# Attention and a two-step expert layer on one core: rows reloaded earlier, gathers one group further ahead, tokens and velocities in one buffer

## The reference

```python
probs = softmax(_gelu(xf @ router_w1 + router_b1) @ router_w2 + router_b2)
topk_p, topk_i = top_k(probs, 2)                   # two of eight experts for each token
v = zeros_like(xf); integrated = xf
for _ in range(2):
    ctx = concatenate([integrated, v], axis=-1)
    x_sh, v_sh = _inl(_gelu(ctx @ shared_w1 + shared_b1) @ shared_w2 + shared_b2, integrated, v, mu)
    ctrl = _experts(ctx_e, flat_idx, expert_w1, expert_b1, expert_w2, expert_b2)
    x_r, v_r = _inl(ctrl, x_e, v_e, mu)            # for both choices, then weighted and summed
    x_next = sw * x_sh + (1.0 - sw) * x_r
    v_next = sw * v_sh + (1.0 - sw) * v_r
    halt = sigmoid(_gelu(integrated @ halt_w1 + halt_b1) @ halt_w2 + halt_b2)
    integrated = integrated + halt * (x_next - integrated)
    v = v + halt * (v_next - v)
refined = _gelu(integrated @ refine_w1 + refine_b1) @ refine_w2 + refine_b2
out = layernorm(xf + (xf + integration_weight * refined))
```

## Time and profile before

| | us |
|---|---|
| median of 3 runs (1504.65 to 1505.9) | 1505.86 |
| the profiled execution, its own time | 1501.05 |
| its span, first to last instruction | 1499.3 |
| VectorE busy in the span | 1052.8 |
| TensorE busy in the span | 1051.0 |
| ScalarE busy in the span | 848.2 |
| GpSimd busy in the span | 500.4 |

### The profile page before, as it was taken

The page is one execution under the profiler, slowest core; times in us unless marked ns, Lnnn a source line. Parts: engine busy times, 40 slices in busy tenths (PEclk is TensorE's granted clock), DMA queues, the critical chain, the costliest instruction groups (busy, mean ns, idle before and its releaser), DMA issues.

```text
span 1499.3 us, 21764 instructions
## 1 busy us (share of the span) xinstructions
PE 1051.0 (70%) x6930; PEld 637.8 (43%) x6930; DVE 1052.8 (70%) x2044; ACT 848.2 (57%) x1307; POOL 500.4 (33%) x604
## 2 busy tenths in 40 slices
PE   4687889798888985671316676166787888835776
PEld 2333545454454543340115454143455566513444
DVE  1575665666666743586647998589987989965777
ACT  1125444354444472544627898256687999954545
POOL 7103222232323232805750000374234434018551
PEclk9769889898989997886558878597788999967889
DMA  4975372818357114951242555585334545233342
GB/s 66 168 97 107 57 110 48 136 43 114 77 79 115 29 41 130 266 172 64 97 138 76 180 187 166 183 262 166 120 113 118 164 127 150 63 104 116 117 120 85
DMA packets 151757, 178.85 MB, mean 119 GB/s; under 512 B 33208, under 2 KB 127827, under 8 KB 151518
## 3 DMA queue, kind: packets, MB, share of 16 engines
q1 hardware_dynamic: 134624, 124.85, 35.8%
q0 software_dynamic: 17024, 52.58, 11.8%
HBM read 100.25 MB, written 76.87 MB: 118 GB/s over the span
## 4 chain that ended last, share of the span: by engine, by line
DVE 18%; ACT 11%; PE 9%; issue 9%; POOL 6%; DMA 6%; SPq 1%; DVEq 0%; POOLq 0%; ACTq 0%
PE exp_ps L2054 3%; POOL xs_dram L1336 3%; ACT ct L1493 2%; ACT ct L1504 2%; PE exp_ps L2032 2%; DVE e_xT L1613 2%; ACT e_xT L1418 1%; ACT L1505 1%; DVE xs L1887 1%; DMA rb<-L_ffn_integration_weight 1%; SPq L1177 1%; DVE rb L1807 1%; DVE rb L1805 1%; DVE vs L1888 1%; POOL xg L1375 1%
## 5 line engine op out<-in xcount | busy, mean ns | idle before, releaser
L543 ACT ACTIVATE probs<-att_ps 128x512 f32<-128x512 f32 x320 | 175.8, 610 | 160.6 <-PE att_ps L783 159.8
L605 DVE TENSOR_REDUCE neg_max<-att_ps 128x1 f32<-128x512 f32 (+3 forms) x448 | 217.0, 533 | 63.4 <-PE att_ps L774 61.8
L773 PE MATMUL att_ps<-k_stack,q_stack 96*128 96x512 bf16 (+3 forms) x512 | 160.7, 355 | 64.4 <-DVE neg_max L605 33.3
L1418 ACT CAST e_xT<-exp_ps 128x512 f16<-128x512 f32 x156 | 84.8, 606 | 122.3 <-PE exp_ps L2032 122.1
L1343 POOL DMA_INDIRECT xg<-rs_dram,pos x64 | 64.8, 1013 | 229.2 <-DMA rs_dram<-rb 182.3
L2054 PE MATMUL exp_ps<-w_top,h_hl 128*128 (+2 forms) x280 | 89.1, 382 | 62.5 <-issue 32.2
L783 PE MATMUL att_ps<-q_stack,k_stack 98*128 98x512 bf16 (+3 forms) x512 | 125.4, 319 | 5.9 <-DMA q_stack<-max_parts 3.7
L774 PE MATMUL att_ps<-mask_q,identb 128*128 128x128 bf16 x512 | 125.1, 250 | 0.0
L2157 PE MATMUL exp_ps<-e_xT,w 128*128 128x128 f16 x432 | 103.7, 242 | 15.2 <-DVE e_xT L1613 13.4
L773 PEld LDWEIGHTS att_ps<-k_stack,q_stack 96*128 96x128 bf16 x512 | 54.1, 108 | 137.0 <-DVE neg_max L605 93.6
L2032 PE MATMUL exp_ps<-e_ident,xs 128*128 128x128 f32 x192 | 36.5, 352 | 106.2 <-DVE vs L1888 45.4
(11 more groups left out here) (275 smaller groups left out, 2799.5 us busy)
## 6 DMA issues: line engine op xcount, KB each, us to landing
rs_dram<-rb SPq DMA_DIRECT2D x18, 1024.0 KB, 4.9
parts_dram<-parts SPq DMA_DIRECT2D x48, 256.0 KB, 2.6
q_stack<-parts_dram SPq DMA_DIRECT2D x96, 128.0 KB, 5.8
k_stack<-parts_dram SPq DMA_DIRECT2D x96, 128.0 KB, 8.4
xs_dram<-zeros SPq DMA_DIRECT2D x18, 520.0 KB, 9.5
xg<-xs_dram SPq DMA_DIRECT2D x18, 520.0 KB, 6.1
rs_dram<-rb SPq DMA_DIRECT2D x18, 512.0 KB, 2.9
x_in<-in_L_attn_encodings SPq DMA_DIRECT2D x8, 512.0 KB, 10.0
```

What stands on the lines that cost most here:

```text
L543: nc.scalar.activation(probs[:, pair % 4, u, :], src, ACT.Exp).then_inc(free, 1)
L605: return v.tensor_reduce(out, scores, AX.X, ALU.max, negate=True)
L773: t_.matmul(out, stationary, moving, start=True, stop=False)
```

## The change

- In the first mix one addition of 128x512 takes the place of two of 128x256: its first half lies in `xs`, its second in `vs`. For this both become parts of one buffer `state`, and `both(t)` names the two halves. The tiles go in pairs: first choice of both tiles, then second choice of both.
- In the second mix all first choices of a group stand before all second choices.
- SyncE loads the rows of group g+2 as soon as take g has freed its PSUM slot (`ctrl_freed`), ahead of the store of group g.
- GpSimd's queue in the refinement becomes: gathers 0, gathers 1, add 0, gathers 2, add 1, gathers 3, gathers 4, add 2, gathers 5, add 3, gathers 6, add 4, gathers 7, adds 5 to 7.

```diff
...
             return ps[:, RINGS + 2 * (n % 2):RINGS + 2 * (n % 2) + 2, :].rearrange("p a n -> p (a n)")
 
 
-        xs = sb("xs", [P, TILES, XW], F32)
-        vs = sb("vs", [P, TILES, D], F32)
+        state = sb("state", [P, TILES * (XW + D)], F32)
+        xs = state[:, 0:TILES * XW].rearrange("p (t n) -> p t n", n=XW)
+        vs = state[:, TILES * XW:].rearrange("p (t d) -> p t d", d=D)
         w1 = sb("w1", [P, 2, 2 * KC, E + 1, 2, HID], F16)
         b1_parts = sb("b1_parts", [P, E * P], F16)
         w2_top = sb("w2_top", [P, (E + 1) * CTRL], F16)
...
         xT32 = [view(xg_flat, 1024 * i, KC, TOK) for i in range(2)]
 
         hl_all = view(xg_flat.bitcast(F16), 2 * 2096, 2 * GROUPS, TOK)
+
+        def both(t):
+            at = t * XW
+            return AP(vs.tensor, at, [list(vs_flat.ap[0]), [TILES * XW + t * D - at, 2], [1, D]])
 
         def sort_view(i):
             return view(vs_flat, 512 * i, E, 2 * TILES)
...
             for g in range(2):
                 load(x1b[g], x_dram[g], x1_full[g])
             for g in range(GROUPS):
+                if g + 2 < GROUPS:
+                    u = uses(EWS) + g
+                    sync.wait_ge(ctrl_freed[u % 2], u // 2 + 1)
+                    load(x1b[g % 2], x_dram[g + 2], x1_full[g % 2])
                 sync.wait_ge(final_ready, g + 1)
                 sync.dma_start(out_dram[g], final).then_inc(final_stored, 16)
-                if g + 2 < GROUPS:
-                    load(x1b[g % 2], x_dram[g + 2], x1_full[g % 2])
             sync.wait_ge(final_stored, 16 * GROUPS)
 
         @block.gpsimd
...
             pool.wait_ge(ew_done, EWS)
             for i in range(2):
                 pool.wait_ge(rs_stored[i], 16 * stores_before(EWS, i))
-            for t in range(2 * NT):
-                gather2(t)
+            def gather_group(g):
+                for t in range(g * NT, (g + 1) * NT):
+                    gather2(t)
+
+            gather_group(0)
+            gather_group(1)
             pool.wait_ge(bias2_scaled, 1)
             residual(0)
-            for g in range(GROUPS):
+            gather_group(2)
+            residual(1)
+            gather_group(3)
+            for g in range(2, GROUPS):
                 if g + 2 < GROUPS:
-                    for t in range((g + 2) * NT, (g + 3) * NT):
-                        gather2(t)
-                if g + 1 < GROUPS:
-                    residual(g + 1)
+                    gather_group(g + 2)
+                residual(g)
 
         @block.scalar
         def _(act):
...
             first_velocity(W_S2 - 1)
 
             def combine1(g):
-                for t in range(g * NT, (g + 1) * NT):
-                    dve.wait_ge(cb_full[t % CBS], 32 * (t // CBS + 1))
+                for pair in range(g * NT, (g + 1) * NT, 2):
                     for k in range(2):
-                        c = nwx[0][:, t, k + 1:k + 2]
-                        v.scalar_tensor_tensor(xs[:, t, 0:D], cb1(t)[:, k, 0:D], c, xs[:, t, 0:D], ALU.mult, ALU.add)
-                        last = v.scalar_tensor_tensor(vs[:, t, :], cb1(t)[:, k, D:], c, vs[:, t, :], ALU.mult, ALU.add)
-                        if k == 0:
-                            last.then_inc(dve_step, 1)
-                            then()
-                    last.then_inc(comb_done, 1)
+                        for t in range(pair, pair + 2):
+                            if k == 0:
+                                dve.wait_ge(cb_full[t % CBS], 32 * (t // CBS + 1))
+                            else:
+                                then()
+                            v.scalar_tensor_tensor(both(t), cb1(t)[:, k, :].rearrange("p (a d) -> p a d", d=D),
+                                                   nwx[0][:, t, k + 1:k + 2], both(t), ALU.mult,
+                                                   ALU.add).then_inc(dve_step if k == 0 else comb_done, 1)
 
             def halts(g):
                 src, free = filled(f"cl{g}")
...
 
             def combine2(g):
                 dve.wait_ge(pairs_moved[g], 2 * 16 * 2 * NT)
-                for t in range(g * NT, (g + 1) * NT):
-                    for k in range(2):
-                        last = v.scalar_tensor_tensor(xs[:, t, 0:D], cb2(t)[:, k, :], nwx[1][:, t, k + 1:k + 2],
-                                                      xs[:, t, 0:D], ALU.mult, ALU.add)
-                        if k == 0:
-                            last.then_inc(dve_step, 1)
+                for k in range(2):
+                    for t in range(g * NT, (g + 1) * NT):
+                        if k:
                             then()
-                    last.then_inc(comb_done, 1)
+                        v.scalar_tensor_tensor(xs[:, t, 0:D], cb2(t)[:, k, :], nwx[1][:, t, k + 1:k + 2],
+                                               xs[:, t, 0:D], ALU.mult, ALU.add).then_inc(dve_step if k == 0 else comb_done, 1)
 
             def refine_low(g):
                 for c in range(RC):
```

More of the change, by code:

```diff
@@ L13 @@
 from concourse import mybir
-from concourse.bass import IndirectOffsetOnAxis, ds
+from concourse.bass import AP, IndirectOffsetOnAxis, ds
 ALU = mybir.AluOpType
```

## The result

The kernel after takes 1483.81 us (median of 4 runs, 1482.61 to 1487.74), the one before 1505.26 (4 runs, 1502.4 to 1505.9). By the medians that is 21.5 us less. The ratio is 0.9866, 95% interval 0.9843 to 0.9888, which is 20.2 us less (16.9 to 23.6); the forecast was 1483. The profiled executions show less: 1483.65 us with a span of 1481.9, against 1501.05 and 1499.3, that is 17.4 less. The profile of before lay 4.2 us under its median, that of after on it. The kernel varies by some us from one execution to the next ahead of the stages of interest (the first gather of the first mix's ring starts anywhere from 953 to 967 us), so the stages are compared by their own lengths.

A forecast was written before the change was run, and what follows sets the result against it. VectorE was taken to bound the first mix; in the refinement it waited for late gathers. −7.2 and −15.9 give −23.1 us, from 1501.05 to 1477.9; with 4.8 added, 1483 us, range 1475 to 1491.

The forecast's parts named there:

- the other: Refinement: gather waits, reordered second mix, adds, late gelus and end were to sum to −15.9 us.
- The first mix: First mix: merged additions take 0.67 us each, saving 1.5 us a group in mixes 3 to 7; −7.2 us in sum.
- The gather waits: Refinement: earlier loads and gathers remove VectorE's waits of 7.16 and 7.56 us; −14.7 us.
- The wait before mix 2: Refinement: VectorE's 5.21 us gather wait stays, since gathers 0 to 2 and adds 0 and 1 stand as before.
- The second mix: Refinement: the reorder removes four 0.12 us gaps a group, 0.45 us each in mixes 2 to 7; −2.7 us.
- The adds: Refinement: GpSimd's adds 2 to 7 hold VectorE 1.4 us each, 8.4 against about 6.5 before; +2.0 us, bounds 0 and +7.6.
- rival 1: Refinement: the adds take everything they can from VectorE, +7.6 us in place of +2.0; 1488 us, chance 0.14.
- late gelus: Refinement: TensorE and ScalarE deliver some low parts after VectorE arrives, about 0.3 us a group; +1.5 us, bounds 0 and 4.
- The end: Mix 7 to take 7 of the refinement: TensorE's clock falls less with shorter gaps; −2.0 us, bounds 0 and −4.
- GpSimd as the bound: Refinement: GpSimd's gathers and adds set the pace, everything else falls well; 1473 us, chance 0.10.
- TensorE at the low clock: Refinement: TensorE stays at the low clock throughout and bounds, making the kernel slower; 1534 us, chance 0.03.

The follow-up runs named there:

- second measurement of the kernel after: The kernel after, unchanged, measured again beside the kernel before on another chip: 1486.59 us, ratio 0.9889.
- second kernel with the old order: The kernel after with the second mix back tile by tile, measured again: 1481.21 us, ratio 0.9828.

## Why the prediction was right

The total was right, with help. The forecast added 4.8 us to the profile's time, because that profile lay under its median. The profile of after did not lie under its own, so by profiles 17.4 us went and not 23.1, and by the ratio of the runs 20.2 (16.9 to 23.6). The second measurement of the kernel after gives 16.7 (10 to 23). One part was right, the other gave about half of what was said: −8.0 where −15.9 stood (−11.9 in the second profile). That 1483 was met within 1 us is luck: the refinement's missing 7.9 us were made up by the 4.8 added, by 1.7 us outside both stages and by 0.5 more in the first mix.

**The first mix, −7.2 expected.** Right in mechanism and size: starts 0.66 apart (0.67 taken), 5.29 us a group (5.3), a period of 17.68 us (17.7). Five periods gave 7.7 us. The figures of the Trainium skill (VectorE: DVE Perf Modes, the section on the TRN2 errata) gave 6.3 us for the five groups, where the trace has 7.7: the rows were rightly preferred.

**The gather waits, −14.7 expected.** Both are gone, as said. That either of the two moves would have done it was not seen.

**The wait before mix 2, 0 expected.** It grew, and mix 2 came 1.8 us later. The step "gathers 0 to 2 and adds 0 and 1 stand as before" looked at the queue alone; the issue of a gather itself became longer, because the reordered mix 1 and the low parts behind it left GpSimd no gap. Why the same four low parts hold a gather for 3.29 us there and for 1.42 us with the old order is open (the last section has the rows).

**The second mix, −2.7 expected.** The mix is shorter by the amount named: 3.24 us for 3.75. From mix 2 to mix 7 that gave 2.6 us. But with the new queue the whole of the edit costs some 7 us in the stage, a little by the long gather and mostly by where the adds then come to lie. This is the term whose sign was wrong, for this queue; for the old queue it was not tried.

**The adds, +2.0 expected, bounds 0 and +7.6.** From mix 2 to mix 7, stretched rows exceed their likes by 10.9 us after (10.5 and 0.4 in mix 2) and by 4.2 before: +6.7, near rival 1. Over all of adds 2 to 7 it is 12.0 after and 6.6 before, +5.4: 2.0 us an add after, where 1.4 was taken. The sum over this stretch closes: −14.7 for the gathers, −0.5 for a wait on ScalarE that went, +1.4 for late gelus (+1.5 expected), −2.6 for the shorter mixes and +6.7 are −9.7, and −9.6 was measured. The mean of the four adds read in the profile of before was taken for a property of the adds. It is one of where they fall: 0.04, 1.3 or 2.5 us for the same 2.35 us of work. The periods from mix 3 to mix 7 show it too: 15.2 us on average, where 13 to 14 were named. Rival 1 took the rule of the Trainium skill (SBUF — State Buffer, "Who interferes with whom") for a worst case, since steps with an input in PSUM are left out. The rows agree with the rule in both directions: the statistics (1.41) and the low parts from PSUM (1.28 for two) run on, the low parts with two inputs in SBUF stand still for the whole add. The 128x4 L86 has a single SBUF input and stands still too (2.71); by that section an operation of its kind may use the shared ports as well.

**The end, −2.0 expected.** 37.3 us before, 37.2 after: nothing. But the second profile of the same program has 34.4, −2.9, and the three with the old order of the second mix 34.9. The first has add 7 beside a low part (2.15 us instead of 0.69), the second lost 0.4 us to it. So the term was about right, and the first profile hid it. Its ground was not quite: the stretch at clock 0.63 begins where the wait of 7.16 us ends. Without any adds it is 34.4 us, so most of it is the chain of a group through TensorE, ScalarE and VectorE.

**The rivals.** GpSimd as the bound did not come, though it was near: it is busy 57.45 of 73.43 us from mix 2 to 7 and stands 0.30 us before most of its gathers, but VectorE waits for none of them behind mix 2. TensorE at the low clock neither: 0.89 of full speed from mix 2 to mix 7, and 0.93 to 0.97 there with the old order of the mix. Why the late gelus and the clock go together there was not separated.

## What to carry over

An elementwise operation on GpSimd costs VectorE what is left of it when VectorE comes to an operation with two SBUF inputs, or to one like L86. So its place in the queue matters more than its length: put it beside work on PSUM, or give it to an engine with time to spare. Before an order is made gapless on VectorE, ask what GpSimd has to issue meanwhile; in the refinement, with the adds and the new queue, the gaps were worth more than the 0.12 us each that they cost, and without the adds they were worth nothing. And where two moves serve one wait, each should be timed alone.

## What was not expected of the hardware

- The issue of a gather, 0.95 us, took 5.00 us beside eight merged additions and the products behind them, and 1.62 us at most (1.96 once) when gaps of about 0.1 us stood between dependent pairs. The Trainium skill (SBUF — State Buffer, "Who interferes with whom") has descriptor generation starved by VectorE's two-port modes and infers that plain two-input operations do not do it. Here each form was enough by itself: the gather of 3.51 us stood beside additions with a scalar per row, that of 3.29 us beside low parts, plain two-input operations.
- A gapless run does not always hold a gather. In the second kernel with the old order one issued at 1369.55, 0.09 us behind the start of the second low part, took 1.42 us beside four low parts (1368.86, 2.49 us) that show no gap either. What decides between 1.4 and 3.3 us was not found.
- A held VectorE row can start 0.3 us ahead of the add's own row (L86 at 1405.97, the add at 1406.28). Either the add takes hold before its row begins or the row begins late; the traces do not tell.
- One profile is not a kernel: the refinement of one and the same program took 147.6 and 143.7 us in two profiles, in part because two adds fell together in one and apart in the other.
